# Attention stages of a transformer: score maxima in pairs of heads, quotients from the sums' bank, side work at new places

## What is computed

```python
def _mha(x, y, wq, wk, wv, li1_w, li1_b, lnx_g, lnx_b, lny_g, lny_b, ln3_g, ln3_b, li2_w, li2_b, li3_w, li3_b, causal):
    xn = _ln(x, lnx_g, lnx_b)
    yn = _ln(y, lny_g, lny_b)
    q = jnp.einsum('bsc,hcd->bhsd', xn, wq)
    k = jnp.einsum('btc,hcd->bhtd', yn, wk)
    v = jnp.einsum('btc,hcd->bhtd', yn, wv)
    a = jax.nn.softmax(jnp.einsum('bhsd,bhtd->bhst', q, k) * D ** (-0.5), axis=-1)
    ...
    o = jnp.einsum('bhst,bhtd->bhsd', a, v)
    o = o.transpose(0, 2, 1, 3).reshape(x.shape[0], x.shape[1], H * D)
    x_out = x + o @ li1_w + li1_b
    ...
```

## Time and profile before

| | |
|---|---|
| Time, median of 3 runs | 8038.13 us (8025.27 to 8046.97) |
| The profiled execution's own time, and its span | 8022.59 us, 8020.8 us |
| TensorE, VectorE, ScalarE, GpSimd busy in the span | 89%, 74%, 62%, 29% |
| Own attention: first to last maximum (L1354) | 3224.1 to 3785.1 us |
| Cross attention: first to last full maximum (L1357) | 3983.4 to 6144.1 us |

### The profile page before, as it was taken

How to read it: one execution, slowest core, us unless ns; L and a number is a source line. 1 busy time by engine, 2 the same in 40 slices (tenths; PEclk the granted TensorE clock), 3 DMA queues, 4 the chain that set the end, 5 groups by cost and what they waited for, 6 DMA issues and landing times. The chain is left out here.

```text
span 8020.8 us, 186125 instructions
## 1 busy us (share of the span) xinstructions
PE 7135.1 (89%) x73814; PEld 3142.3 (39%) x73814; DVE 5918.4 (74%) x12885; ACT 4951.6 (62%) x9846; POOL 2313.2 (29%) x2368
## 2 busy tenths in 40 slices
PE   6999999878999997888599999999998779999979
PEld 2333333353333333444244444444444533333335
DVE  6888888657989996677466666666665469899855
ACT  4778887636888884444255555555554248888852
POOL 1222222111121110444245444544444211221200
PEclk9999999888999998788699999999999779999989
DMA  4444333114433421000100000000000144434400
GB/s 97 101 95 92 83 83 92 45 26 100 99 89 77 99 65 31 15 16 13 53 6 8 7 6 10 6 10 6 7 3 18 49 83 96 96 84 85 97 22 14
DMA packets 319828, 417.80 MB, mean 52 GB/s; under 512 B 56533, under 2 KB 238053, under 8 KB 318968
## 3 DMA queue, kind: packets, MB, share of 16 engines
q1 hardware_dynamic: 317432, 405.36, 22.4%
q10 hardware_dynamic: 1536, 0.53, 0.0%
HBM read 225.41 MB, written 174.66 MB: 50 GB/s over the span
## 5 line engine op out<-in xcount | busy, mean ns | idle before, releaser
L687 ACT ACTIVATE a_probs<-scores_ps 128x512 f32<-128x512 f32 (+2 forms) x5248 | 2821.7, 591 | 356.2 <-PE scores_ps L607 263.4
L746 DVE TENSOR_REDUCE a_unit_max<-bank 128x1 f32<-128x512 f32 x3072 | 2004.0, 684 | 182.0 <-PE bank L594 147.3
L624 PE MATMUL bank<-a_probs,a_v_sb 128*9 128x256 f32 (+1 forms) x20992 | 1614.1, 379 | 29.4 <-ACT a_out_sb L694 20.4
L1275 ACT ACTIVATE cross_probs<-scores_ps 128x512 f32<-128x512 f32 (+1 forms) x1792 | 869.4, 571 | 772.6 <-PE scores_ps L1172 772.6
L1357 DVE TENSOR_REDUCE cross_unit_max<-bank 128x1 f32<-128x512 f32 x1536 | 1006.5, 687 | 319.7 <-PE bank L1158 316.9
L607 PE MATMUL scores_ps<-a_stack 64*128 64x256 bf16 (+1 forms) x10496 | 1131.5, 275 | 61.6 <-ACT a_probs L687 55.8
L1441 POOL TENSOR_TENSOR cross_added<-cross_probs 128x1024 f32<-128x1024 f32 x384 | 902.4, 2350 | 944.6 <-PE bank L1205 868.8
L746 DVE TENSOR_REDUCE a_unit_max<-scores_ps 128x1 f32<-128x512 f32 x1536 | 1050.2, 684 | 162.1 <-PE scores_ps L594 144.6
L594 PE MATMUL bank<-a_stack 63*128 63x512 bf16 (+2 forms) x3413 | 1039.7, 372 | 8.1 <-DMA a_stack<-a_stack_dram 2.6
L607 PEld LDWEIGHTS scores_ps<-a_stack 64*128 64x128 bf16 (+1 forms) x10496 | 373.5, 96 | 991.9 <-ACT a_probs L687 832.8
L594 PE MATMUL scores_ps<-a_stack 63*128 63x512 bf16 (+2 forms) x1707 | 635.9, 373 | 50.8 <-DMA a_stack<-a_stack_dram 47.5
(11 more groups left out here) (421 smaller groups left out, 10119.5 us busy)
## 6 DMA issues: line engine op xcount, KB each, us to landing
a_stack_dram<-a_parts SPq DMA_DIRECT2D x288, 400.2 KB, 4.3
a_stack<-a_stack_dram SPq DMA_DIRECT2D x256, 348.2 KB, 8.0
a_stack<-a_stack_dram SPq DMA_DIRECT2D x128, 444.2 KB, 9.9
a_ctxT<-in_ctxT SPq DMA_DIRECT2D x48, 400.2 KB, 4.9
a_stack_dram<-a_parts SPq DMA_DIRECT2D x288, 64.0 KB, 2.7
a_stack_dram<-a_parts SPq DMA_DIRECT2D x96, 128.0 KB, 2.8
f_x<-x_after_dram SPq DMA_DIRECT2D x32, 256.0 KB, 3.6
x_after_dram<-a_res SPq DMA_DIRECT2D x48, 128.0 KB, 4.6
```

The costliest lines, as they stand in the source:

```text
L624: ins = pe.matmul(out_bank[32 * h:32 * h + V8, q0:TOK], v[0:n, e.t, 4 * e.g + h, :], A.probs[0:n, held, o + q0:o + TOK], start=(e.t == 0), ...
L687: act.activation(by_pair(A.probs[0:n, b, a * 512:(a + 1) * 512])[:, :, q0:TOK], by_pair(score_bank[(2 * e.i + a) % 3][0:n, :])[:, :, q0:TO ...
L746: ins = dve.tensor_reduce(unit_max[:, e.g % 2, qt, 2 * a + j, c:c + 1], bank[:, 0:e.s.chunks[c][1]], AX.X, ALU.max)
L1275: act.activation(probs[0:n, b, h, 0:m, :].rearrange("p m q -> p (m q)"), score_bank[h][0:n, 0:m * TOK], ACT.Exp, scale=scale).then_inc(S[" ...
```

## The change

- **Pairs of heads.** Units 2n and 2n + 1 are a pair: two heads, one in each maximum bank (`unit32` picks the head by the bank's number). The banks become one tensor `max_ps`, and VectorE takes both with one maximum of 1024 elements, at the second unit (`max_taken` + 2). A pair may be written when the pair before has been taken. This holds for own as well.
- **Places.** `PAIRS32` sets the pairs of a quad by step and part (0 ahead of the value product, 1 ahead of the sums, 2 at the end): two full pairs in most steps, one in the short step at place 1; the small units stand at place 5, ahead of the last full pair. Values, keys, q and turns now all stand in slot 1, one per step at most: values in steps 3, 9, 10, 16, 17, 23, 24, first half of keys at place 4, q at 5, second half of keys at 0 of the next quad, turn at 6. Layer norm and transposes of the inputs stand earlier; the output projection in step 2 in place of 3. In own the units are 2 + 2 in place of 2 + 1 + 1.
- **Quotients from the bank.** In cross there is no ScalarE copy to `out_sb`: VectorE's reciprocal and product read `out_bank`, and the first value product of the next quad waits for that product.

```diff
@@ -838,6 +838,8 @@
 LN_PIECES = 5
+PAIRS32 = ((-1, ((0, 0), (2, 2))), (0, ((0, 4), (2, 6))), (1, ((0, 8),)), (2, ((0, 10), (2, 12))), (3, ((0, 14), (2, 16))),
+           (4, ((0, 18), (2, 20))), (5, ((0, 24), (1, 26), (2, 22))))
@@ -853,13 +855,14 @@
-    def unit32(self, k):
+    def unit32(self, k, u):
+
+        head = k % 4 // 2 * 2 + u % 2
         if self.own:
-            return k, None, 0
+            return head, None, 0
...
-        return k % 4, k // 4 % QT, k // 4 // QT
+        return head, k // 4 % QT, k // 4 // QT
@@ -899,24 +902,25 @@
             for j in range(LN_PIECES):
-                put((4, 5, 11, 12, 12)[j], 1, "ln_stats", j=j)
-                put((14, 15, 16, 17, 18)[j], 2, "ln_apply", j=j)
-            put(12, 2, "ln_rstd")
-            for j in range(2):
-                put(20 + j, 0, "ctx", j=j)
-            put(23, 0, "x_turned")
-        for j, (i, slot) in enumerate(((4, 0), (8, 0), (8, 2), (11, 0), (15, 0), (15, 2), (22, 0))):
-            prepare(i, slot, True, "v", j=j)
+                put((0, 4, 5, 6, 6)[j], 1, "ln_stats", j=j)
+                put(8 + j, 2, "ln_apply", j=j)
+            put(6, 2, "ln_rstd")
+            put(15, 1, "ctx", j=0)
+            put(19, 2, "x_turned")
+            put(22, 1, "ctx", j=1)
+        for j, i in enumerate((3, 9, 10, 16, 17, 23, 24)):
+            prepare(i, 1, True, "v", j=j)
         for quad in range(1, QUADS + 1):
             g, base, nxt = quad % QUADS, per_quad * (quad - 1), quad == QUADS
-            prepare(base - 3, 2, nxt, "q", g=g)
-            for c in range(2):
-                prepare(base - 2, 2 * c, nxt, "k", g=g, c=c)
-            slots = [i for i, n in ((-1, 5), (0, 5), (2, 5), (3, 5), (4, 4), (5, 4)) for _ in range(n)]
-            for k in range(s.NU):
-                prepare(base + slots[k], 0, nxt, "unit", g=g, k=k, r=int(k == s.NU - 1))
-            prepare(base + 6, 0, nxt, "turn", g=g)
-        proj_at = (3, 2)
+            prepare(base - 3, 1, nxt, "k", g=g, c=0)
+            prepare(base - 2, 1, nxt, "q", g=g)
+            prepare(base, 1, nxt, "k", g=g, c=1)
+            for rel, places in PAIRS32:
+                for part, first in places:
+                    for k in (first, first + 1):
+                        prepare(base + rel, 0, nxt, "unit", g=g, k=k, part=part, r=int(k == PAIRS32[-1][1][-1][1] + 1))
+            prepare(base + 6, 1, nxt, "turn", g=g)
+        proj_at = (2, 2)
@@ -926,17 +930,17 @@
-        first = 1 if any(e.kind in "kv" and not s.own for e in at.get((i, 0), [])) else 2
-        plan += at.get((i, 0), []) + units[0:first]
+        by_part = [[e for e in units if e.part == part] for part in range(3)]
+        plan += at.get((i, 0), []) + by_part[0]
...
-        plan += units[first:first + 1] + at.get((i, 1), [])
+        plan += by_part[1] + at.get((i, 1), [])
...
-        plan += units[first + 1:]
+        plan += by_part[2]
@@ -1180,7 +1186,7 @@
                     if e.takes:
-                        pe.wait_ge(S["heads_out"], e.takes)
+                        pe.wait_ge(S["heads_out" if own else "normed"], e.takes)
@@ -1274,7 +1280,7 @@
-                if e.kind == "take":
+                if e.kind == "take" and own:
                     act.wait_ge(S["sums"], e.summed)
@@ -1347,15 +1353,16 @@
                     dve.wait_ge(S[f"max_scores{e.u % 2}"], e.u // 2 + 1)
-                    if qt is None:
-                        ins = dve.tensor_reduce(unit_max[:, e.g % 2, :, h, c], bank[:, 0:QT * n].rearrange("p (t n) -> p t n", t=QT),
-                                                AX.X, ALU.max)
-                    else:
-                        ins = dve.tensor_reduce(unit_max[:, e.g % 2, qt, h, c:c + 1], bank[:, 0:n], AX.X, ALU.max)
-                    ins.then_inc(S["max_taken"], 1)
+                    if e.k % 2:
+                        if qt is None:
+                            ins = dve.tensor_reduce(unit_max[:, e.g % 2, :, pair, c].rearrange("p t h -> p h t"),
+                                                    max_banks[:, :, 0:QT * n].rearrange("p h (t n) -> p h t n", t=QT), AX.X, ALU.max)
+                        else:
+                            ins = dve.tensor_reduce(unit_max[:, e.g % 2, qt, pair, c], max_banks[:, :, 0:n], AX.X, ALU.max)
+                        ins.then_inc(S["max_taken"], 2)
@@ -1372,11 +1379,15 @@
                 if e.kind == "norm":
-                    dve.wait_ge(S["heads_out"], e.takes)
+                    if own:
+                        dve.wait_ge(S["heads_out"], e.takes)
+                    else:
+                        dve.wait_ge(S["sums"], e.summed)
...
+                    heads = out_sb[:, e.g % 2, :] if own else out_bank
+                    chain(dve.reciprocal(inv[:, :], heads[:, TOK:2 * TOK]))
+                    dve.tensor_tensor(attnT[:, of_set(e), e.g, :], heads[:, 0:TOK], inv[:, :], ALU.mult).then_inc(S["normed"], 1)
@@ -2374,7 +2385,9 @@
-        G.bank = [ctx.enter_context(nc.psum_tensor(f"bank{i}", [P, 512], F32)) for i in range(4)]
+        G.M2 = ctx.enter_context(nc.psum_tensor("max_ps", [P, 2, 512], F32))
+        G.bank = [ctx.enter_context(nc.psum_tensor(f"bank{i}", [P, 512], F32)) for i in range(2)]
+        G.bank += [G.M2[:, 0, :], G.M2[:, 1, :]]
```

More of the change, by code:

```diff
@@ L854, in __init__ @@
         self.NU = 4 if own else QT * 4 * self.full + 4
-    def unit32(self, k):
+    def unit32(self, k, u):
+        head = k % 4 // 2 * 2 + u % 2
         if self.own:
-            return k, None, 0
+            return head, None, 0
         if k >= QT * 4 * self.full:
-            return k - QT * 4 * self.full, None, self.full
-        return k % 4, k // 4 % QT, k // 4 // QT
+            return head, None, self.full
+        return head, k // 4 % QT, k // 4 // QT
 def segment32(s, cur):
@@ L893, in segment32 @@
             for k in range(s.NU):
-                prepare(step, 0, not late, "unit", g=g, k=k, r=int(k == s.NU - 1))
+                prepare(step, 0, not late, "unit", g=g, k=k, part=k // 2 * 2, r=int(k == s.NU - 1))
             prepare((g + 3) % QUADS, 0, g == 0, "turn", g=g)
@@ L964, in schedule32 @@
         if e.kind == "begin":
-            e.after = side.get(("x_turned", 0, e.cur + 1))
+            e.after = side.get(("x_turned" if s.own else "ctx", 0, e.cur + 1))
         if e.kind == "ln4":
@@ L980, in schedule32 @@
         if e.kind == "unit":
-            h, qt, c = s.unit32(e.k)
+            h, qt, c = s.unit32(e.k, e.u)
             e.cast = cast[e.g, e.batch, "k", c // 2]
+            if not s.own:
+                e.cast = max(e.cast, cast[e.g, e.batch, "q", 0])
             e.last = e.r == 1
@@ L1004, in schedule32 @@
             e.takes = takes
+            e.summed = summed[e.i]
     return plan
@@ L1038, in heads32 @@
         added = sb("added", [P, ADDS32, 4, TOK])
-        out_sb = sb("out_sb", [P, 2, 2 * TOK])
+        out_sb = sb("out_sb", [P, 2, 2 * TOK]) if own else None
         inv = sb("inv", [P, TOK])
@@ L1049, in heads32 @@
         score_bank = [G.S4[:, h // 2, h % 2, :] for h in range(4)]
-        out_bank, side_bank, max_bank = G.bank[0], G.bank[1], G.bank[2:4]
+        out_bank, side_bank, max_bank, max_banks = G.bank[0], G.bank[1], G.bank[2:4], G.M2
         n_tiles = T + QT
@@ L1349, in program_dve @@
                 if e.kind == "unit":
-                    h, qt, c = s.unit32(e.k)
-                    n, bank = s.chunks[c][1], max_bank[e.u % 2]
+                    h, qt, c = s.unit32(e.k, e.u)
+                    n, pair = s.chunks[c][1], slice(h // 2 * 2, h // 2 * 2 + 2)
                     dve.wait_ge(S[f"max_scores{e.u % 2}"], e.u // 2 + 1)
-                    if qt is None:
-                        ins = dve.tensor_reduce(unit_max[:, e.g % 2, :, h, c], bank[:, 0:QT * n].rearrange("p (t n) -> p t n", t=QT),
-                                                AX.X, ALU.max)
-                    else:
-                        ins = dve.tensor_reduce(unit_max[:, e.g % 2, qt, h, c:c + 1], bank[:, 0:n], AX.X, ALU.max)
-                    ins.then_inc(S["max_taken"], 1)
+                    if e.k % 2:
[5 more added lines that the diff above has]
+                        ins.then_inc(S["max_taken"], 2)
                     if e.last:
@@ L1374, in program_dve @@
                 if e.kind == "norm":
-                    dve.wait_ge(S["heads_out"], e.takes)
+                    if own:
+                        dve.wait_ge(S["heads_out"], e.takes)
+                    else:
+                        dve.wait_ge(S["sums"], e.summed)
                     if e.takes > 1:
                         dve.wait_ge(S["normed"], e.takes - 1)
-                    chain(dve.reciprocal(inv[:, :], out_sb[:, e.g % 2, TOK:2 * TOK]))
-                    dve.tensor_tensor(attnT[:, of_set(e), e.g, :], out_sb[:, e.g % 2, 0:TOK], inv[:, :], ALU.mult).then_inc(S["normed"], 1)
+                    heads = out_sb[:, e.g % 2, :] if own else out_bank
```

(2 more changed lines are left out.)

1 line of the change is left out of this document (removed).

## The result

The changed kernel takes 8098.56 us (median; 8085.51 to 8105.47), the kernel before, run beside it, 8034.78 (8025.27 to 8046.97). The ratio is 1.0077 (95%: 1.0057 to 1.0096): slower by 0.8%, 64 us between the medians. The range of the prediction (7975 to 8160) holds it; the forecast, 8051 us and no change that can be told, does not.

The account below looks back on a forecast made before the run. The prediction took TensorE to bound the cross stage, its savings returning as waits on VectorE. Terms -25 + 22 + 9 + 7 = +13 us on a median of 8038.1 gave 8051 us, no change that can be told; range 7975 to 8160.

Parts of the forecast that it names:

- the dear maximum: Slower rival: VectorE's maximum over two banks takes 1.37 us, not 1.23; +95 us, 8150 us; chance 0.16 together with another wait.
- the lower bound: Shortest time allowed for VectorE's maximum over 1024 elements: 1.08 us, if no start-up were left; 1.23 was taken.
- The bound and the mechanism: Cross stage bound by TensorE; its 9 us saved per batch come back nearly whole as waits on VectorE through the banks.
- 9 of occupied time: Cross units in pairs occupy TensorE 2.2 us less per quad, 9 per batch.
- pair to the next pair: .43 + 1.23 + .15 = 1.81: Cross hand-over: pair start to its maximum .43, maximum 1.23, its end to the next pair .15 us.
- 134.5: Forecast cross batch in us from the summed links, against 136.15 before; -1.6 per batch, -25 us in all.
- +22: Cross stage: if the lower clock's share stays, slower links cost 1.4 us per batch x 15.5 = +22 us.
- The faster rival: Shorter long stops in cross remove the lower clock's +22, and hand-overs .03 shorter give 20 more: 8009 us; chance 0.25.
- The slower rival by clock: Cross attention's granted clock falls to 0.84 as in own attention, through more TensorE stops: +150, 8200 us; chance 0.17.
- The estimate of 8 us: Reciprocal and product reading the bank would be .13 us longer, 64 times, by the skill page; left out of the sum.
- Start of the stage: First quads of cross: pairs take 2.03 us against 1.45 for two units, 16 pairs x .58 = +9 us.
- Own stage: Own attention: joint maxima behind the reciprocal delay row maxima, +11, less 4 in TensorE-bound steps: +7 us.

Follow-up runs that it names:

- the run with the copy back: The changed kernel, but in cross attention ScalarE copies heads and sums out of their bank again and quotients come from that copy: 8142.8 us, a batch 143.8.
- one semaphore: The changed kernel, but in cross attention a pair's units count up one semaphore, so the maximum carries one wait, not two: 8065.39 us, a batch 140.1.
- kernel with single maxima: The changed kernel, but in cross attention each unit has its own maximum and frees its own bank; own stage stays as changed: 7826.56 us, a batch 125.7.

## Where the prediction held and where it failed, point by point

- **The range** (7975 to 8160) holds 8098.56, and that is in part luck: its upper end stood for the dear maximum (1.37 us), which did not come, while the loss comes from the start-up of the links, to which the range gives nothing of its own. (Its lower end is also mis-summed: half-way to the lower bound is .075 us per maximum, 7958; 7975 goes with .05.) The forecast of 8051, within 0.3%, missed by 48.
- **The bound and the mechanism** were right: two banks freed by one instruction are one buffer, and what TensorE saves comes back as waits. Its busy time per batch fell by 5.0 (125.80 to 120.75), where I had 9 of occupied time, and its idle time rose by 9.6. 1.23 us for the maximum was right; the rival of the dear maximum is out.
- **The step that failed is the sum of the links, in its first term: "pair to the next pair: .43 + 1.23 + .15 = 1.81".** The .43 was taken from a lone unit whose bank was free; the pair, which waits for its banks, has .63 (.51 behind its second unit). The projection follows the maximum in .14, not .06; the kernel before has .15 there as well, in all 62 places in which its key projection waits for a maximum, so this was a misreading and not a surprise. Places measured (medians) against forecast: 0 5.41 (5.06), 1 and 2 with values 9.1, or 9.5 to 9.6 with a context turn (8.9 and 9.15), 3 5.79 (5.57), 4 5.89 (5.57), 5 4.57 (4.33), 6 4.29 (4.06). That is some 1.5 in a quad that has all of them. Without the lower clock's share (.7, next point) a batch is 140.9, not 134.5: 6.4 x 15.5 = +99 us. The value product's wait for the quotients (37.3 us, 45 times, about .8), which I had held to lie within VectorE's chain, does appear; the run with the copy back trades it for a later reciprocal and is no faster, so what it costs by itself is not shown.
- **The clock** was mis-sized in the other direction: in 4155 to 6045 us the lower level held 85 us before and 45 after, not an equal share; by the prediction's own price 1.4 us a batch became .7, and +22 about +11 (an estimate). The faster rival was right in its premise (fewer long stops, 0.98 -> 0.99) and wrong in its sum, since it took the links to be shorter. The slower rival by clock did not come: some 34 stops per batch, of .4 to .8 on average by kind (the four rows of waits above), leave it at 0.99. It has come in the run with both the old places and shared banks, 0.91, with stops of up to 2.2 us. The Trainium skill (page "TensorE: Matmul & The Clock Gate", section "A second HAM failure mode: psum-queue depth-cycling") describes a kernel that cycles through banks with small stops and whose clock swings. This last run bears it out; the changed kernel, which cycles through its banks with small stops just so, bears out little of it, since its clock falls in short spells that add up to half of what they did before.
- **Quotients**: right in direction, and in "no dearer from a bank" (reciprocal 1753 ns from the bank, 1753 from the copy; product 425 and 425). The estimate of 8 us worked out from the Trainium skill (page "VectorE: DVE Perf Modes", section "The TRN2 errata") has no trace here. But I gave the edit no term of its own, and alone it is -3.6 per batch in the kernel before (-65 us): this part pays without the others.
- **Start of the stage** +9, measured +7: from the first maximum to the first scores 31.5 us before, 38.7 after (the +8 above has a part of the first batches in it). **Own stage** +7, measured 0 in the profile, within its scatter.
- Corrected: 13 + 99 - 11 (clock) - 7 (own) - 2 (start) = +92 against +77 in the profiles; the earlier start of the stage (8) and the shorter work behind it (5) make 13 of the difference, 2 are left.

What I did not see at all: the parts pull apart. In this order, before 136.2 -> quotients -3.6 -> pairs -.4 -> places -6.4 -> both banks in one +15.9, about 141.6. Three of four parts gain 10.4 us a batch, and the last one loses them all and 5.5 more. In another order the shares would differ: quotients bring 2.2 and the places 9.8 (151.4 to 141.6, clock included) where the banks are shared. The kernel without the joint maximum, 7826.56 us, beats both before and after.

## To carry to other kernels

One instruction that empties two buffers makes them one, and here that cost more than three gains brought: before doing so, hold the whole link (fill, start-up, work, release) against what the producer has to do in the meantime, at each place where two fills follow each other. Take the parts of the link from rows in which the same pattern occurs, a pair behind a wait and not a lone unit with a free bank, and where no row shows it, put the difference between the nearest rows into the range of every link, times their number. A change of several parts is summed part by part: here the whole moved +0.8%, and its two halves -2.4% (all but the joint maximum) and +3.5% (the joint maximum).

## What the runs showed of the hardware

- A pair of matmuls in different row groups: started together (.39) when both banks are free, .12 apart when they waited. The maximum that reads both starts .55 and .63 behind the first matmul in the changed kernel (medians of 145 and 303 links in 4155 to 6045 us), .52 and .60 with one semaphore; that of a lone matmul .42.
- One maximum over two banks costs no more than 9 ns beyond its elements: 128x2 from 128x512 over two banks 693 ns, 128x1 from 128x512 in one bank 684.
- One spell of 3.4 us at the lower clock cost a batch 1.2 us (kernel with single maxima: 126.6 in the four batches that hold one in the same step, 125.4 in the nine that hold none).
- Between the starts of its first and last row maximum the own stage takes 531 to 534 us in five profiled executions, at a clock of 0.87 to 0.88; 559 to 563 in eight, at 0.81 to 0.83; and 549 in one, at 0.84. The two groups don't follow the edits: after, with the joint maxima in this stage, lies in the longer one (its row stands above, 0.82) beside before, with single ones, and the kernel with single cross maxima, whose own stage is that of after, in the shorter:

```profile
3224.00:3780.00 556.00, 433.82 (x4814) 235.84 (x4814) 410.21 (x745) 272.17 (x508) 267.83 (x282) 0.88 0.06 16
```

What sets the one or the other isn't settled. The 28 us between them are why differences below some 30 us of whole time are read from batches here.
